# A convolution stage with 24 shared tiles, rotated output matmuls and a reload in halves; the image first on the queue; no block of its own for clearing semaphores

## The reference

```python
x = x + L0_conv(_gn(x))      # linear attention per image, with 4 memory keys
x = x + L1_conv(_gn(x))      # depthwise convolution, 51 x 51 kernel per channel, padding 25
t = _to_tokens(x)            # 32 x 256 tokens of 32 numbers
t = t + L2_attn(_ln_t(t))    # 4 layers of linear attention, 8 heads
t = t + L2_ffn(_ln_t(t))     # mixture of 8 experts, 2 chosen
t = t + L3_attn(_ln_t(t))    # squared attention
t = t + L3_ffn(_ln_t(t))     # up to 33 steps of blocks chosen by an argmax
```

## Time and profile before

| what | value |
|---|---|
| median of 3 runs | 697.68 us (690.64 to 698.04) |
| profiled execution | 689.62 us, span 687.8 us |
| TensorE busy | 571.4 us, 83% of the span |
| VectorE busy | 415.5 us, 60% |
| ScalarE busy | 303.6 us, 44% |
| GpSimd busy | 119.0 us, 17% |
| first load to end of linear attention | 0 to 92.6 us |
| second norm and convolution | 92.9 to 169.6 us |
| linear transformer | 169.9 to 245.1 us |
| clearing block | 245.1 to 249.2 us |
| all that follows | 249.2 to 687.8 us |

### The profile page before, as it was taken

The page is one execution under the profiler, slowest core; times in us unless marked ns, Lnnn a source line. Parts: engine busy times, 40 slices in busy tenths (PEclk is TensorE's granted clock), DMA queues, the critical chain, the costliest instruction groups (busy, mean ns, idle before and its releaser), DMA issues. The chain is left out here.

```text
span 687.8 us, 15220 instructions
## 1 busy us (share of the span) xinstructions
PE 571.4 (83%) x6332; PEld 349.2 (51%) x6336; DVE 415.5 (60%) x671; ACT 303.6 (44%) x452; POOL 119.0 (17%) x217
## 2 busy tenths in 40 slices
PE   0675789998899969888788877968999899899983
PEld 0555644673799836324555554433654465355420
DVE  2679775711412335786688875745686668557663
ACT  0356544110332211105788885325555455645563
POOL 0133420000000000003355650000222023112200
PEclk9897999999899987998999998978999999999998
DMA  7300041013000006400000000000000000000002
GB/s 224 35 2 2 4 186 17 1 31 91 1 1 1 1 2 143 102 1 1 1 2 2 2 2 18 0 8 11 2 1 2 11 1 2 10 2 2 1 6 65
DMA packets 23987, 17.15 MB, mean 25 GB/s; under 512 B 17354, under 2 KB 22506, under 8 KB 23275
## 3 DMA queue, kind: packets, MB, share of 16 engines
q1 hardware_dynamic: 23194, 13.54, 8.5%
q10 hardware_dynamic: 720, 2.56, 1.0%
HBM read 9.76 MB, written 2.13 MB: 17 GB/s over the span
## 5 line engine op out<-in xcount | busy, mean ns | idle before, releaser
L1911 DVE TENSOR_REDUCE R<-ps 128x4 f32<-128x1024 f32 x48 | 57.7, 1212 | 30.8 <-PE ps L1499 30.8
L1746 ACT ACTIVATE R<-ps 128x1024 f32<-128x1024 f32 x48 | 49.1, 1023 | 52.9 <-PE ps L1510 52.9
L1302 POOL TENSOR_TENSOR R<-R 128x512 f32<-128x512 f32 x32 | 45.3, 1417 | 49.1 <-DVE R L1238 49.1
L1920 DVE RECIPROCAL R<-R 128x256 f32<-128x256 f32 x24 | 41.9, 1746 | 14.9 <-ACT R L1739 14.9
L1510 PE MATMUL ps<-tmpA,R 32*128 32x256 f32 x384 | 49.5, 374 | 0.0
L1238 DVE TENSOR_TENSOR R<-ps,lasting 128x512 f32<-128x512 f32 x64 | 41.2, 686 | 12.6 <-PE ps L1170 12.6
L1499 PE MATMUL ps<-R,tmpA 32*128 32x256 f32 x384 | 47.7, 400 | 0.0
L1271 ACT ACTIVATE R<-R 128x1536 f32<-128x1536 f32 x32 | 47.3, 1478 | 0.1
L1170 PE MATMUL ps<-R,Q 32*128 32x128 f32 (+1 forms) x512 | 30.5, 351 | 15.0 <-ACT R L1287 15.0
L85 PE MATMUL ps<-lasting 128*128 128x512 f32 x72 | 36.5, 666 | 3.9 <-DVE R L140 2.8
L1510 PEld LDWEIGHTS ps<-tmpA,R 32*128 32x128 f32 x384 | 37.2, 184 | 0.7
(11 more groups left out here) (301 smaller groups left out, 1213.7 us busy)
## 6 DMA issues: line engine op xcount, KB each, us to landing
R<-z SPq DMA_DIRECT2D x16, 256.0 KB, 5.1
R<-in_qv SPq DMA_DIRECT2D x1, 2560.0 KB
x<-in_x SPq DMA_DIRECT2D x4, 256.0 KB, 7.2
scratch_x<-R SPq DMA_DIRECT2D x8, 128.0 KB, 2.2
Q<-scratch_x SPq DMA_DIRECT2D x1, 1024.0 KB, 5.6
out<-x SPq DMA_DIRECT2D x4, 256.0 KB, 2.7
lasting<-in_lasting ACTq DMA_DIRECT2D x1, 811.0 KB
early<-in_early ACTq DMA_DIRECT2D x1, 793.5 KB
```

Source lines behind the costliest of these rows:

```text
L1302: pool.tensor_tensor(diagonal(u), diagonal(u), diagonal(u), ALU.mult).then_inc(diag_squared[1], 1)
L1746: act.activation(m.et[:, g % 2, 2 * i:2 * i + 2, :], ps[:, 4:6, :], ACT.Exp).then_inc(sg["exp_done"], 1)
L1911: dve.tensor_reduce(m.mx[:, g, 2 * a:2 * a + 4], ps[:, a:a + 2, :].rearrange("p i (s m) -> p (i s) m", s=S), AXX, ALU.max).then_inc(sg["ma ...
L1920: dve.reciprocal(m.yz[:, g, N:2 * N], m.yz[:, g, N:2 * N]).then_inc(sg["inv_done"], 1)
```

## The change

The first block loads x and then all tables on SP's queue; `kpe` is loaded in the attention's block, on SP's queue ahead of its class tables. The first block ends after the statistics: z is made at the head of the attention's block, where ScalarE squares groups 0 to 5 straight from x (scale and bias from `inv8` and a new `shift8`) and VectorE squares groups 6 and 7 from z. TensorE gets `keep_busy` of eight matmuls on a cleared `tmpA` in the first block. Waits are split by table (`tables_loaded`, `early_loaded`, `lasting_loaded`). The product `wvo` is made after the first round of key maxima instead of at the start, and value rounds come one key round later.

The second norm moves into the convolution's block (transposes follow z group by group). T has 24 tiles, since a half's Toeplitz rows are the other half's, shifted: the eight tiles in the middle serve both halves. They are copied by ScalarE; the other sixteen are copied by VectorE with `kmat` added on the way, so `kmat` remains as a matmul only for the middle ones, 128 columns wide for each half. The output matmuls are ordered by step first and by strip second. Stores and reload go in halves, with parts of the second half on ScalarE's queue. The clearing block goes; GpSimd clears spent semaphores in three later blocks.

```diff
-def keep_busy(pe, m, bank, n):
+def keep_busy(pe, m, bank, n, what=None):
+    t = m.lasting if what is None else what
     for _ in range(n):
-        pe.matmul(m.ps[:, bank, :], m.ident[:, :], m.lasting[:, 0:CH], start=True, stop=True)
+        pe.matmul(m.ps[:, bank, :], t[:, 0:128], t[:, 0:CH], start=True, stop=True)
...
@@ linear_attention @@
-            for k in range(NCH):
-                pe.wait_ge(squared, k + 1)
-                for g in (2 * k, 2 * k + 1):
-                    mm = gather_squares(pe, m, 4, m.tmpB, g, g == 0, g == G - 1)
+            pe.wait_ge(m.tables_loaded, 16 * 2)
+            for g in range(G):
+                if g < BY_ACT:
+                    pe.wait_ge(squared, g + 1)
+                else:
+                    pe.wait_ge(squared_v, g - BY_ACT + 1)
+                mm = gather_squares(pe, m, 4, m.tmpB, g, g == 0, g == G - 1)
...
             key_maxima_round(0)
+            pe.wait_ge(wo_spread, 1)
+            pe.matmul(ps[:, 7, 0:128], m.wvt[:, :], m.wobd[:, :], start=True, stop=True)
+            pe.matmul(ps[0:MEM, 7, 128:256], m.memvt[:, :], m.wobd[:, :], start=True, stop=True).then_inc(wvo_ready, 1)
+            pe.wait_ge(m.lasting_loaded, 16 * 2)
+            key_maxima_round(1)
+            pe.wait_ge(wvo_made, 2)
             value_round(0)
-            key_maxima_round(1)
+            key_maxima_round(2)
             value_round(1)
-            key_maxima_round(2)
             key_maxima_round(3)
             value_round(2)
...
@@ peripheral_convolution @@
-    NT = H * S
+    HR = H // S
+    NT = H + HR
+    norm = second_norm(m, sem, d)
+    order = [(t, by_act) for i in range(HR) for t, by_act in ((i, False), (HR + i, True), (H + i, False))]
...
+            keep_busy(pe, m, 7, 5)
             for q in range(NCH):
+                pe.wait_ge(norm.done, 2 * (q + 1))
                 for i in range(4):
...
-                for cc in range(4):
-                    c = 4 * ci + cc
-                    o = ps[32 * cc:32 * cc + 32, (4 + ci) % 8, 0:N]
-                    for s in range(S):
-                        lhsT = zt[:, s * G * 128 + c:(s + 1) * G * 128:C]
-                        rhs = T[:, s, :, :].rearrange("p y (c x) -> p y c x", c=C)[:, :, c, :]
-                        pe.matmul(o, lhsT, rhs, start=(s == 0), stop=False)
-                        mm = pe.matmul(o, lhsT, m.kmat[:, s, :], start=False, stop=(s == S - 1))
+                for step, half in (("own", 0), ("shared", 0), ("shared", 1), ("own", 1)):
+                    for cc in range(4):
+                        c = 4 * ci + cc
+                        o = ps[32 * cc:32 * cc + 32, (4 + ci) % 8, 0:N]
+                        lhsT = zt[:, half * G * 128 + c:(half + 1) * G * 128:C]
+                        if step == "own":
+                            first = HR * (1 - half)
+                            rhs = T[:, first:first + H, :].rearrange("p y (c x) -> p y c x", c=C)[:, :, c, :]
+                            mm = pe.matmul(o, lhsT, rhs, start=(half == 0), stop=(half == 1))
+                        else:
+                            cols = slice(half * HR * W, (half + 1) * HR * W)
+                            pe.matmul(o[:, cols], lhsT, m.kmat[:, half, cols], start=False, stop=False)
...
-                dve.tensor_copy(T[:, s, y, :], ps[:, w % 4, :]).then_inc(t_copied_v, 1)
+                dve.tensor_tensor(T[:, t, :].rearrange("p (c x) -> p c x", c=C),
+                                  ps[:, w % 4, :].rearrange("p (c x) -> p c x", c=C),
+                                  m.kmat[:, half, None, y * W:(y + 1) * W].broadcast_to([128, C, W]),
+                                  ALU.add).then_inc(t_copied_v, 1)
...
-            sp.wait_ge(out_stored, 8 * 16)
-            sp.dma_start(m.tmpB[:, :].rearrange("p (g n) -> p g n", g=G),
-                         m.scratch_x.rearrange("(g j) c n -> (j c) g n", j=J)).then_inc(out_loaded, 16)
+            sp.wait_ge(out_copied, 4)
+            for cc in range(4):
+                store(sp, 0, cc)
+            sp.wait_ge(out_stored[0], 4 * 16)
+            for j in range(J):
+                reload(sp, 0, j)
+            sp.wait_ge(out_copied, 8)
+            for cc in range(2):
+                store(sp, 1, cc)
+            sp.wait_ge(out_stored[1], 4 * 16)
+            for j in range(2):
+                reload(sp, 1, j)
...
+            act.wait_ge(out_copied, 8)
+            for cc in range(2, 4):
+                store(act, 1, cc)
+            act.wait_ge(out_stored[1], 4 * 16)
+            for j in range(2, J):
+                reload(act, 1, j)
...
+        @block.gpsimd
+        def _(pool):
+            norm.pool(pool)
+            for spent in m.spent[0]:
+                pool.sem_clear(spent)
...
@@ load_first @@
+            keep_busy(pe, m, 7, 8, m.tmpA)
...
+            act.activation(m.warm[:, :], m.eps[0:1, 0:1], ACT.Sqrt)
...
-                if not last:
-                    with nc.Block() as block:
-                        @block.gpsimd
-                        def _(pool):
-                            for s in sems[0::4]:
-                                pool.sem_clear(s)
...
```

More of the change, by code:

```diff
@@ L589, in _ @@
         def _(sp):
+            for s in range(S):
+                for y in range(H // S):
+                    first = KS // 2 - R
+                    src = toeplitz_rows(d.kpe, (first + y + (S - 1 - s) * (H // S)) * KS + first, 1,
+                                        (W, [[KS, H], [1, W]]))
+                    sp.dma_start(m.kmat_rev[16 * y:16 * y + 16, s, :].rearrange("p (y x) -> p y x", y=H),
+                                 src).then_inc(m.loaded_kpe, 16)
             sp.wait_ge(classes, CLASSES)
@@ L669, in _ @@
         def _(sp):
+            norm.sp(sp)
             sp.wait_ge(turned_copied, 1)
@@ L694, in _ @@
                 mm.then_inc(yt_ready, 1)
-            pe.matmul(ps[:, 4, :], m.exchange[:, :], m.kmat_rev[:, :, :].rearrange("p s n -> p (s n)"),
-                      start=True, stop=True).then_inc(turned, 1)
-            for w in range(NT):
-                y, s = divmod(w, S)
+            pe.wait_ge(norm.cast, 6)
+            pe.wait_ge(norm.left, 4)
+            for w, (t, _) in enumerate(order):
+                half, y = source(t)
                 if w < 4:
@@ L702, in _ @@
                 else:
[L703 removed]
+                    wait_tile(pe, w - 4)
                 for i in range(3):
[L705 removed]
+                    mm = pe.matmul(ps[:, w % 4, :], m.onehot[half][:, (R - y) * W:(R - y + 8) * W], m.bparts[half][:, i, :],
                                    start=(i == 0), stop=(i == 2))
                 mm.then_inc(t_ready, 1)
[L708 to L709 removed]
+            for n in range(NT - 4, NT):
+                wait_tile(pe, n)
             pe.wait_ge(rel_loaded, 16 * S)
@@ L729, in _ @@
         def _(act):
+            norm.act(act)
             for q in range(NCH):
@@ L884, in _ @@
                 mm.then_inc(out_ready, 1)
+        @block.gpsimd
+        def _(pool):
+            for spent in m.spent[1]:
+                pool.sem_clear(spent)
         @block.vector
@@ L2226, in leave @@
             pool.tensor_tensor(m.bparts[s][:, 2, :], rest[s], m.bparts[s][:, 1, :], ALU.subtract).then_inc(left, 1)
-    instance_norm(nc, m, sem, "gn1", m.x, m.z, None, start, first_parts, leave, second_parts,
-                  lambda pe: keep_busy(pe, m, 7, 8))
+    norm = Mem()
+    norm.sp, norm.dve, norm.act, norm.pool = run_sp, run_dve, run_act, run_pool
+    norm.done, norm.cast, norm.left = done, cast, left
+    return norm
 def prepare(dve, m, made):
```

305 lines of the change are left out of this document (168 added, 137 removed).

## The result

| | median | range | runs |
|---|---|---|---|
| before | 696.57 us | 690.64 to 698.04 | 4 |
| changed | 662.13 us | 657.72 to 665.97 | 4 |

A forecast was written before the change was run, and what follows sets the result against it. It took x's arrival to bound the start and TensorE the convolution's outputs. Terms summing to 41.5 us took the profiled 689.6 to 648.1; 2 added for the timed runs' level gave 650 us, own range 642 to 658, whole range 640 to 666.

The forecast's parts named there:

- rival 1: Convolution outputs: the strips still run two at a time, 22.9 us instead of 13.0, total 658 to 660 us; chance 0.15.
- Outputs: Convolution's output matmuls: neighbours write different strips, so the stretch takes 13.0 us instead of 30.5, -17.5 us.
- rival 4: Convolution outputs: rotating strips exposes each weight load and matmul in full, slower than before, 768 us; chance 0.02.
- Tiles: Convolution's T: 8 fewer tiles at 0.65 us each, TensorE staying the bound, -5.2 us.
- rival 3: Convolution tiles: VectorE becomes the bound, 17.6 us instead of 15.6, total 652 us; chance 0.05.
- rival 2: Table loads at the start: one queue is slower than two, 4 us lost, total 654 us; chance 0.07.
- To xn: First block and first norm up to product xn: xn 7.5 us earlier, 1.3 lost in the maxima, net -6.2 us.
- Store and reload: After the convolution's outputs: halves on two queues take 10.4 us from last matmul through add instead of 12.2, -1.8 us.
- the first transformer start: First products behind the reload (L116): shorter idle time before them keeps TensorE's clock full, -1.7 us.
- the clearing: Boundary between the two transformers: the 4.06 us clearing block becomes an ordinary block end of 0.3, -3.8 us.
- the second start: L116 products behind the former clearing block: shorter idle time keeps TensorE's clock full, 6.54 us to 3.5, -3.0 us.
- Rival 5: Any stage: a block still ends on something else, or the clock falls elsewhere as often as saved, 655 us; chance 0.06.

## Why the prediction was right, and where it missed

Predicted 650 us in 640 to 666; measured 662.13. The direction, the main term and most of the places were right. The size was less so: 662.13 is above the forecast's own range of 642 to 658, and it lies in the whole range by the room that was given to the level of the timed runs and to rival 1 (658 + 8), which did not come true. That it lies inside is in part luck. The sum was 7 us too large by the medians (-34.4 for -41.5), and I had started it from 689.62 us where before has its median at 696.57. Of the 12 us between forecast and measurement, the level that I started from accounts for 5 (6.95, of which I had added 2), the sum for 7.

**Steps that held.** *Outputs*: -19.9 us measured over the stretch (31.5 to 11.6) for -17.5. The outputs took 10.4 us for 13.0. The rate of L432 in the earlier trace rows, 57 ns for 256 columns, was the right neighbour: the order alone, on the kernel before, gave 55, and the changed kernel's own groups 54. The instructions of 128 columns were cheaper than I took them, 27 ns each for 37, and the microsecond that I added for the strided weights was not there. Rival 1 falls, and so does rival 4. The Trainium skill's page "TensorE: Matmul & The Clock Gate" ("Why this matters for your kernels") says of narrow outputs to put each in another group of columns; the runs agree, with 119 / 55 = 2.2 times here. *Tiles*: 24 at 0.65, and rival 3 falls with VectorE busy for 10.87 of 16.70 us. *Second norm*: -2.1 for -2.3. *Queue*: both tables were there in time, rival 2 falls.

**The first step that missed: "To xn", -6.2, was -2.85 at the last maximum and -3.3 at the end of the attention stage.** Of the 3.35 us that are missing at the maximum, 1.9 are the rounds. I put 1.3 us on the wvo work in VectorE's chain and value rounds one key round later; it was 18.7 - 15.5 = 3.2 us, and 2.7 of it came back when both were undone. Two stalls came, of 1.61 and 1.09 us, 2.7 together where I had allowed 0 to 1.5. The other 1.45 us lie ahead of `xn`: the block ended 0.7 us later than my 10.8, and at the lower clock the spread (L64) took 3.69 us instead of 2.01, so that VectorE waited 2.04 us where I took 1.24. The warm-up did not keep the clock: the granted clock was at 0.50 (1.2 GHz) from 13.7 us on.

**The second: "Store and reload", -1.8, was +1.7, and the first transformer start, -1.7, was +1.4.** I had the last reload issued 3.2 us behind the last output matmul (0.5 + 2.7) and the add 4.7 us behind that (0.4 + 4.3); it was 5.8 and 5.6. The larger miss, 2.6 us, is the issue: SP was still issuing the first half's reload when the second half's stores were due, and they landed beside it. I had named this as a possible loss, but within a gain of 0.5 to 2.5 us. The run with the old order, in which the same code issues its reload after 3.8 us, shows that the fast outputs bring it about. The other 0.9 us is the rate. I had priced half a megabyte at 411 GB/s; with the DMA engines as busy it went at 149 to 241, and the half took as long from issue to add as the whole megabyte before (5.7 us). TensorE was idle for 4.5 us behind its dummy products, longer than before (2.85 in the earlier trace rows), and the condition of the next term, a shorter idle time, was not met. The first subtraction came 4.9 us after the add's start as before; the eight products took 6.59 us, and 5.27 and 6.72 in the two other profiles of this code, for 5.23 before. So the +1.4 is one profile's.

The Trainium skill's page "DMA: Bandwidth & Descriptors" ("Rules for kernel authors"), which I had cited as speaking against the split, was right by this case's runs: one transfer was 2.3 us better at the add. Its first line, which asks for 128 partitions and at least 1 MiB per transfer for the most bandwidth, names the smaller part of what I missed; 386 against 149 to 241 GB/s agree with it, without telling the partitions from the size. Half did go while TensorE still worked, as I had argued, but it held up the other half.

**The third: the clearing, -3.8, and the second start, -3.0.** At their place both came true for the engine: 4.1 us became 0.3, and the eight products take 3.67 us, 2.9 less. VectorE's first subtraction gained less of the latter, 0.9 us (1.1 us behind the products' start for 2.1). Whether they reach the end was not settled: 0 and 6.5 us on two bases, for 6.8 forecast.

**A term that was missing: the clock of the stages that the change doesn't touch.** The sum of stages up to the mixture's first subtraction is 251.3 - 219.2 = 32.1 us; the profiled spans differ by 23.6, as the unchanged code behind it took 8.5 us longer at 0.91 than at 0.94. Rival 5 names it ("the clock falls elsewhere as often as it is saved", 655 us), with 0.06. Two profiles look like it, that without the warm-up and that in which TensorE kept working: each gained 0.9 to 1.7 us at its place, and little or none of it was left at the mixture. But the unedited code alone gives 440.8 to 445.0 us for the same stretch, so how much of the 8.5 us the change brings about stays open. The medians, which take in that spread, have the change at 34.4 us.

## What to carry to other kernels

Where matmuls write a few output partitions, count their pitch and look for the same form elsewhere in the trace: putting the strip's index innermost took 119 ns to 55, and on the kernel before that one loop gave 19.3 us, over half of what the large change gave. When a stage becomes faster, ask what queue its results now arrive at: a reload sent ahead can stand in front of the stores that follow it. A transfer's rate is to be read from a row with the same number of partitions and the same size. On a kernel that is bound by TensorE, a saving at one place is to be believed by timed medians of several runs, since the clock of the code behind it moves by as much as a small edit is worth; work that is only there to keep TensorE warm is a thing to try without: neither run on it here showed a gain from it at the end.

## What was not expected of the hardware

- DMA engines at a share of 1.03 to 1.16 moved 149 to 241 GB/s to 16 partitions per transfer, and 386 GB/s to 128 partitions in one transfer of 1 MB.
- The clock column says 1.00 in a run's first microseconds whatever TensorE does: in the run without a warm-up the 64 products of L64 took 3.69 us at 15.0 us with 1.00 beside them. That is what they took in the changed kernel with 0.50 beside them, and 2.01 us in the kernel before.
- Sixteen full-size products up to 11.2 us did not keep the clock through what followed, 1.0 us of idle time, then 64 small products (L50), 1.2 us of idle time and 64 more (L64): it stood at 0.50 from 13.7 to 30.8 us, 17.1 us in one piece. In the other eight runs that begin like this it fell too, for 10.2 to 20.5 us.
- Two executions of the same code differ by over 4 us in one stretch of 440 us, TensorE's clock alone being different.
